# An attention and expert kernel on one core: scores and values in offset groups, and a new order at both ends

## What is computed

```python
scores = einsum('bhpqd,bhpkd->bhpqk', qb[:, :, rows], kb[:, :, cols]) * HEAD_DIM ** -0.5
ob = einsum('bhpqk,bhpkd->bhpqd', softmax(scores), vb[:, :, cols])
acc = segment_sum(ob, rows)
x = x + acc @ Wo.T
```

```python
masked = xf[None] * one_hot(argmax(softmax(xf @ gate_w.T))).T[:, :, None]
h = relu(einsum('end,edh->enh', masked, w1) + b1)
routing_output = (einsum('enh,ehd->end', h, w2) + b2).sum(0)
shared = relu(xf @ sw1 + sb1) @ sw2 + sb2
```

## Time and profile before

| | us |
|---|---|
| median of three runs | 916.06 |
| lowest, highest | 911.68, 916.23 |
| the profiled execution | 914.49 |
| its span, first to last instruction | 912.7 |
| TensorE busy in the span | 798.9 (88%) |
| VectorE busy | 593.8 (65%) |
| ScalarE busy | 497.3 (54%) |
| POOL busy | 429.5 (47%) |

### The profile page before, as it was taken

How to read it: one execution, slowest core, us unless ns; L and a number is a source line. 1 busy time by engine, 2 the same in 40 slices (tenths; PEclk the granted TensorE clock), 3 DMA queues, 4 the chain that set the end, 5 groups by cost and what they waited for, 6 DMA issues and landing times.

```text
span 912.7 us, 24404 instructions
## 1 busy us (share of the span) xinstructions
PE 798.9 (88%) x8374; PEld 665.8 (73%) x8374; DVE 593.8 (65%) x1248; ACT 497.3 (54%) x1150; POOL 429.5 (47%) x780
## 2 busy tenths in 40 slices
PE   3465777788999999999999999999999999989894
PEld 3333756577886869697878788787879697868794
DVE  4457577576757777685858676767677686745331
ACT  2264453636565575746575656556574756465452
POOL 2667333342536364554536363637364554455311
PEclk8576998999999999999999999999999999999997
DMA  6669221263624544544535353444444444414730
GB/s 193 185 194 304 69 86 35 81 206 96 199 79 123 161 138 144 159 141 140 170 115 196 114 166 125 145 140 136 161 128 151 149 144 136 148 49 140 239 109 23
DMA packets 97387, 128.19 MB, mean 140 GB/s; under 512 B 14655, under 2 KB 82623, under 8 KB 97088
## 3 DMA queue, kind: packets, MB, share of 16 engines
q1 hardware_dynamic: 89760, 107.89, 38.4%
q0 software_dynamic: 6624, 18.95, 6.2%
q10 hardware_dynamic: 960, 0.79, 0.4%
HBM read 90.80 MB, written 37.04 MB: 140 GB/s over the span
## 4 chain that ended last, share of the span: by engine, by line
PE 62%; DVE 14%; DMA 9%; issue 4%; ACT 4%; POOL 2%; SPq 2%; ACTq 1%; DVEq 0%; POOLq 0%
PE hid L533 16%; PE acc L724 14%; PE nd L638 11%; PE work L533 6%; PE work L622 5%; DVE nmax L1176 4%; PE work L666 3%; DVE PT L1219 2%; PE work L589 2%; DMA QP<-scratch_m 2%; DVE T L1192 2%; DVE check L1187 1%; DMA scratch_q<-T 1%; PE work L542 1%; DMA scratch_m<-mT 1%
## 5 line engine op out<-in xcount | busy, mean ns | idle before, releaser
L1442 POOL TENSOR_TENSOR hl<-h,hh 128x256 fp32r<-128x256 f32 x228 | 169.0, 744 | 326.1 <-ACT hh L982 325.9
L966 ACT ACTIVATE PT<-work 128x512 f32<-128x512 f32 x192 | 106.3, 605 | 55.6 <-PE work L622 55.5
L1195 DVE RECIPROCAL T<-nd 128x256 f32<-128x256 f32 x51 | 89.4, 1753 | 37.9 <-PE nd L638 32.8
L724 PE MATMUL acc<-w_hi,hh 128*128 128x256 f32 (+1 forms) x528 | 112.5, 295 | 0.0
L982 ACT ACTIVATE h<-hid,bias 128x256 f32<-128x256 f32 x144 | 69.1, 480 | 74.7 <-PE hid L533 74.7
L533 PE MATMUL hid<-Xs,W 128*128 128x256 f32 x816 | 109.6, 288 | 0.2
L533 PEld LDWEIGHTS hid<-Xs,W 128*128 128x128 f32 x816 | 102.9, 195 | 2.6 <-DVE Xs L1129 0.7
L724 PE MATMUL acc<-w_lo,hh 128*128 128x256 f32 (+1 forms) x528 | 104.7, 280 | 0.0
L533 PE MATMUL hid<-Xr,W 128*128 128x256 f32 x768 | 104.1, 285 | 0.0
L533 PEld LDWEIGHTS hid<-Xr,W 128*128 128x128 f32 x768 | 94.1, 188 | 5.1
L638 PE MATMUL nd<-PT,V 128*32 128x256 f32 x1024 | 84.0, 401 | 11.5 <-DVE T L1192 5.3
(11 more groups left out here) (191 smaller groups left out, 1651.5 us busy)
## 6 DMA issues: line engine op xcount, KB each, us to landing
W<-w1q SPq DMA_DIRECT2D x64, 512.0 KB, 5.8
KP<-scratch_k SPq DMA_DIRECT2D x192, 64.0 KB, 2.4
QP<-scratch_q SPq DMA_DIRECT2D x180, 64.0 KB, 2.3
scratch_k<-T SPq DMA_DIRECT2D x16, 512.0 KB, 3.5
scratch_q<-T SPq DMA_DIRECT2D x16, 512.0 KB, 3.2
yt<-yq SPq DMA_DIRECT2D x17, 260.0 KB, 2.8
xt<-xq SPq DMA_DIRECT2D x17, 256.0 KB, 3.8
xin<-x SPq DMA_DIRECT2D x16, 256.0 KB, 3.5
```

The source lines that it names most:

```text
L724: mm = nc.tensor.matmul(acc[:, t, :], R(h[:, u % 2, a, P * t:P * t + P]), R(row), start=first, stop=u == UNITS - 1 and h is hl and a == 1, ...
L966: nc.scalar.activation(PT[:, j % 4].rearrange("p t q -> p (t q)"), score_bank(j), ACT.Exp).then_inc(sem["exp_done"], 1)
L1195: nc.vector.reciprocal(T[:, p, :], nd[:, p % 2, 1, :]).then_inc(sem["inverted"], 1)
L1442: nc.gpsimd.tensor_tensor(R(hl[:, u % 2, a]), h32[:, u % 2, a], hh[:, u % 2, a], ALU.subtract).then_inc(sem["hl_done"], 1)
```

## The change

In iterations with a tile, scores and values come in groups: the scores of pairs 2g+1 and 2g+2, then a half of an expert, then the values of pairs 2g and 2g+1. The head sum is done in two halves, the first before the down half that it followed, the second between the two score visits of the next iteration. `ranks` goes behind `shared_down(n, 1)`.

In iterations 0 to 2: the context split of sequence 1 goes ahead of the weight splits; `SPLITS_AT` has another place, in iteration 1, with the last four pieces, which use slots 2, 3, 4, 3; pieces 5, 7 and 9 have their low half made by VectorE; TensorE waits for pieces 6 and 7 in place of all 24 ahead of iteration 1, and for the last one ahead of the first `table`; `make_constants` goes behind quotient 3, and TensorE waits for the load of the constants; `shared_up(n, 3)` goes ahead of the query projection, with its relu; `table` goes behind `front_v`; SP's residual load goes behind the spreads.

At the tail: the load of the tile's tokens goes behind the second of four weight loads (it was last), and `finish_shared` ahead of one `last_low`.

```diff
-SPLITS_AT = (4, 0, 0, 0, 0, 2, 2, 1, 1, 1, 1, 1, 1, 1, 1, 3, 5)
-SLOTS = [n % STAGES for n in range(W1_PIECES + W2_PIECES)]
+SPLITS_AT = (4, 0, 0, 0, 0, 4, 2, 1, 1, 1, 1, 1, 1, 1, 1, 2, 0, 4)
+ON_VECTOR = (5, 7, 9)
+SLOTS = [n % STAGES for n in range(W1_PIECES + W2_PIECES - 4)] + [2, 3, 4, 3]
...
         def low_done(n):
-            return sem["stage_lo"], n + 1
+            return (sem["stage_lo_dve" if n in ON_VECTOR else "stage_lo_pool"],
+                    sum((m in ON_VECTOR) == (n in ON_VECTOR) for m in range(n + 1)))
...
                     load_w1(W1[:, 1], expert, u)
-                    if u == 0 and not at:
+                    if u == (1 if at else 0):
                         sp.wait_ge(sem["x_queued"], 32 * (m + 1))
                         load_tile_x(m, row)
...
-                if at:
-                    sp.wait_ge(sem["x_queued"], 32 * (m + 1))
-                    load_tile_x(m, row)
...
-                if type(i) is int and i == 0:
-                    sp.wait_ge(sem["consts_read"], 1)
-                    load_residual(0, first=True)
-                else:
+                if tile:
                     load_residual(i)
...
                         spread(half)
+                if type(i) is int and i == 0:
+                    sp.wait_ge(sem["consts_read"], 1)
+                if not tile:
+                    load_residual(i, first=type(i) is int and i == 0)
...
                     if type(i) is int and i == 0:
-                        pe.wait_ge(sem["consts_read"], 1)
+                        pe.wait_ge(sem["consts_loaded"], 16 * 9)
...
+            def attention_out(i, more, c):
+                bank = claim(i, ("at", 0), more) if c == 0 else work[:, BANK["at", 0], :]
...
                 pe.wait_ge(sem["y_done"], e + 1)
+                if e == 0:
+                    pe.wait_ge(*low_done(len(pieces) - 1))
...
                 if shared:
+                    shared_down(n, 1)
                     ranks(n, claim(i, ("rk", 0), tile=tile))
-                    shared_down(n, 1)
...
                     expert = None
+                    if shared:
+                        shared_up(n, 3)
                 if more:
                     front_project(i + 1, "q", 0, a_hi, a_lo, "xT_lo", tile=tile)
...
-                elif shared:
-                    shared_up(n, 3)
                 scores_t(i, 0, more)
-                for p in range(PAIRS):
-                    if not tile and p % 2:
+                for p in range(0 if tile else PAIRS):
+                    if p % 2:
                         fill(n, m, tile, (p + 1) // 2, expert)
                     if p + 1 < PAIRS:
                         scores_t(i, p + 1, more)
-                    if tile and p % 2 == 0 and (more or p > 2):
-                        fill(n, m, tile, p // 2, expert)
                     values(i, p)
+                for group in range(GROUPS if tile else 0):
+                    for p in (2 * group + 1, 2 * group + 2):
+                        if p < PAIRS:
+                            scores_t(i, p, more)
+                    if more or group > 1:
+                        fill(n, m, tile, group, expert)
+                    values(i, 2 * group)
+                    values(i, 2 * group + 1)
+                attention_out(i, more, 0)
                 if tile:
                     tile_down(m, 1, expert)
-                elif shared:
-                    table(i - 1)
-                attention_out(i, more)
-                if more:
+                    if more:
+                        scores(i + 1, 0)
+                attention_out(i, more, 1)
+                if more and tile:
+                    scores(i + 1, 1)
+                elif more:
                     visit(i + 1, 0)
...
                     front_v(i + 1)
+                if shared and not tile:
+                    table(i - 1)
...
             iteration(0, False, False, True)
-            pe.wait_ge(*low_done(len(pieces) - 1))
+            pe.wait_ge(*low_done(6))
+            pe.wait_ge(*low_done(7))
...
             def splits(i, k):
-                if type(i) is int and i == 0:
+                if type(i) is int and i == (k == 17):
                     for n in slot_pieces(k):
                         split_high(n)
...
-                if more and not shared:
-                    context_high(i + 1)
+                    if u == 1:
+                        splits(i, 17)
...
+                elif shared:
+                    shared_relu(n, UNITS - 1)
                 splits(i, 6)
...
             front_v(0, acc[:, :, :])
+            context_high(1)
             for n in slot_pieces(0):
                 split_high(n)
...
+            def split_low(n):
+                dve.wait_ge(sem["stage_hi"], n + 1)
+                _, hi, lo = pieces[n]
+                nc.vector.tensor_tensor(R(lo), stage(n, lo), hi, ALU.subtract).then_inc(sem["stage_lo_dve"], 1)
...
+                if type(i) is int and i == 0:
+                    split_low(ON_VECTOR[0])
+                    split_low(ON_VECTOR[1])
                 if more:
                     front_q(i + 1)
                 if type(i) is int and i == 0:
-                    make_constants()
+                    split_low(ON_VECTOR[2])
...
                     divide(i, p)
...
+                    if type(i) is int and i == 0 and p == 3:
+                        make_constants()
...
+            finish_shared(last)
             last_low(tile_unit(last, 0), 0)
-            finish_shared(last)
...
             def split_and_load(n):
-                split_low(n)
+                if n not in ON_VECTOR:
+                    split_low(n)
...
-                if more:
+                splits(i, 17)
+                if more and shared:
                     context_low(i + 1)
...
                 load(n)
+            context_low(1)
             for n in slot_pieces(0):
                 split_and_load(n)
```

More of the change, by code:

```diff
@@ L114 @@
     "table_hi level_hi "
-    "bias_summed consts_made consts_read proj_lo ln1_step ln1_done ln2_step ln2_done xT_lo q_lo k_lo "
+    "bias_summed consts_made consts_read proj_lo stage_lo_dve ln1_step ln1_done ln2_step ln2_done xT_lo q_lo k_lo "
     "max_done m_lo inverted checked t_done at_lo x1_done gate_step masked ranked x2_lo xr_lo y_done r_done "
     "level_sum level_made ids_moved last_low "
-    "zeroed stage_lo veps1_done veps2_done rstd1_done rstd2_done c_lo hl_done table_lo "
+    "zeroed stage_lo_pool veps1_done veps2_done rstd1_done rstd2_done c_lo hl_done table_lo "
     "place_step placed left_made pad_made"
@@ L641, in values @@
                 mm.then_inc(sem["pv_done"], 1)
[L643 to L654, removed]
+            def attention_out(i, more, c):
+                bank = claim(i, ("at", 0), more) if c == 0 else work[:, BANK["at", 0], :]
+                bank = bank.rearrange("p (c t) -> p c t", c=DC)
+                pe.wait_ge(sem["t_done"], PAIRS * i + 4 * c + 4)
+                for r in range(NBLK):
+                    queries = slice(BLOCK * r, BLOCK * r + BLOCK)
+                    for q in range(4):
+                        mm = nc.tensor.matmul(bank[32 * q:32 * q + 32, c, queries], hsum[:, r, :],
+                                              T[:, 4 * c + q, queries], start=True, stop=True)
+                if c == DC - 1:
+                    mm.then_inc(sem["at_full"], 1)
             def project_out(i, more):
@@ L1045, in iteration @@
                     tile_relu(m, 1)
-                elif shared and not tile:
-                    shared_relu(n, UNITS - 1)
                 exps(i, 0)
@@ L1536, in split_low @@
                 _, hi, lo = pieces[n]
-                nc.gpsimd.tensor_tensor(R(lo), stage(n, lo), hi, ALU.subtract).then_inc(sem["stage_lo"], 1)
+                nc.gpsimd.tensor_tensor(R(lo), stage(n, lo), hi, ALU.subtract).then_inc(sem["stage_lo_pool"], 1)
             def split_and_load(n):
-                split_low(n)
+                if n not in ON_VECTOR:
+                    split_low(n)
                 if SLOTS[n] in SLOTS[n + 1:]:
```

## The result

The changed kernel takes 920.22 us (median of 20 runs, 914.47 to 925.62) and the kernel before 915.78 (20 runs, 911.12 to 918.73): ratio 1.0056, 95% interval 1.0035 to 1.0077, about 5 us slower. The forecast was 914.0, no change that counts.

A forecast was written before the change was run, and what follows sets the result against it. TensorE was taken as the bound, busy 563.6 of 585 us at full clock in the tile iterations. Terms +7.8 - 0.5 - 2.3 - 3.0 - 4.0 = -2.0 gave 914.0 us against the 916.06 median; range 903 to 924.

The forecast's parts named there:

- the tail: After the tile iterations: earlier token load saves 2.6 us, earlier finish_shared 1.4; together -4.0, ends -1 and -4.4.
- Tile iterations: Twelve iterations with a tile of routed tokens: +0.65 us each from grouping, head sum and ranks, together +7.8.
- Groups +1.4: Joined scores and values in each tile iteration: new waits outweigh savings, +1.4 us, ends -1.05 and +2.0.
- pair 2's 1.3: First group of a tile iteration: pair 2's scores wait 1.3 us for exponentials of pair 0, whose banks they take.
- pair 4's 0.15: Second group: other TensorE work covers all but 0.15 us of pair 4's wait for pair 2's exponentials.
- pair 6's 0.7: Third group: pair 6's scores wait 0.7 us because F1's relu precedes pair 4's exponentials on ScalarE.
- The joins: Tile iterations: joining saves 0.21 us per pair of scores and 0.14 per pair of values, at most 1.05 per iteration.
- Ranks -0.5: Tile iterations: shared_down(1) covers the 0.77 us mask wait, late maxima then limit it; -0.5, ends 0 and -0.77.
- Head sum -0.25: Tile iterations: splitting it covers 0.34 us more of the last-quotient wait, less 0.1; -0.25, ends 0 and -0.7.
- Rival B: Faster: only pair 2 waits, groups cost +0.7, full mask gain; total -9.8, 906 us, chance 0.35.
- Rival C: Slower: the new 1.3 us wait drops the clock, costing 1.5 us per affected iteration; 926 at eight, chance 0.22.
- Front: Iterations 0 to 2: -2.3 us up to iteration 1's key projection, -3.0 in the rest of iterations 1 and 2.

The follow-up runs named there:

- the second execution: Both kernels run once more, unchanged, one profiled execution each: the kernel before 913.17 us, the changed kernel 927.12 us.
- the tail alone: The kernel before with only the tail's two moves (token load ahead of two weight loads and the bias, finish_shared one unit earlier): ratio 1.0031.

## Why the prediction was wrong

**The step that failed is the tail**: "The two weight loads behind it come some 6 us later, needed later still. -2.6. finish_shared one unit earlier: the 1.5 for yp, -1.4. Together **-4.0**". Alone it measured +2.8, outside its ends of -1 and -4.4, a miss of 6.8 us. Put 2.8 in its place and the sum of the prediction is +4.8 instead of -2.0; measured were 5.1 by the ratio.

The wait for yp is gone, as forecast. The wait for the tokens shrank from 2.88 to 1.90 only, 1.0 for a forecast of 2.6, and "under 1" was missed. The scatter ahead of the load was to land sooner under half the weights; it took 6.48 instead of 6.95, and the load itself 2.87 instead of 3.35. From the chain that ended last, changed kernel:

```profile
854.23 6.48 DMA xq<-xhat,pos
...
860.86 2.87 DMA xt<-xq
```

That alone would have left a gain of about 2.5. What turned it into a loss, and what I did not count, is what stands next on the sync queue. SyncE's queue in the kernel before:

```profile
855.82 0.38 SPq L370 DMA_DIRECT2D xt<-xq  x1
857.03 0.42 SPq L486 DMA_DIRECT2D xq<-T  x1
...
862.09 1.79 SPq L366 DMA_DIRECT2D W<-w1q  x4
864.14 0.39 SPq L370 DMA_DIRECT2D xt<-xq  x1
```

and in the changed kernel:

```profile
860.86 0.38 SPq L372 DMA_DIRECT2D xt<-xq  x1
861.43 0.85 SPq L368 DMA_DIRECT2D W<-w1q  x2
862.47 0.33 SPq L399 DMA_DIRECT2D bsel<-b  x1
863.63 0.42 SPq L486 DMA_DIRECT2D xq<-T  x1
...
869.33 2.14 SPq L368 DMA_DIRECT2D W<-w1q  x4
871.73 0.44 SPq L372 DMA_DIRECT2D xt<-xq  x1
```

The second token load goes out 8.32 us after the first before and 10.87 after: two weight loads and the bias now stand between them, ahead of the padding writes and the four weight loads that stood there already. In the changed kernel it goes out about 0.2 after the last padding write has landed, which took 4.3 instead of 2.7; before, that write had landed over 1 us earlier. Its landing, from the transfers by issue (KB each, us to landing), in the kernel before:

```profile
xt<-xq SPq DMA_DIRECT2D x1, 256.0 KB, 6.7
```

and in the changed kernel:

```profile
xt<-xq SPq DMA_DIRECT2D x1, 256.0 KB, 8.3
```

Before, the tokens landed at 870.81 and were used at 871.60: 0.8 to spare (0.7 in the second execution). That was in the trace before the change, and it means that of any gain ahead of that point only 0.8 could be kept unless the tokens landed earlier too. Counted from the first transposes they now land 4.7 us later (16.29 instead of 11.59), while TensorE arrives 1.5 us earlier (10.87 instead of 12.38). It waits 5.46 and then runs at the lower clock: from the second transposes to the third 14.47 us instead of 12.07, 2.4 more. With the tokens ahead of the weights, in the tail alone, the wait is gone. The transfer there:

```profile
xt<-xq SPq DMA_DIRECT2D x1, 256.0 KB, 2.8
```

Its issue comes only 0.8 us sooner than in the tail alone without that edit (67.82 for 68.59 after the maxima of iteration 15); the landing, 2.8 instead of 7.7 after it, is what the place in the queue is worth. Whether that comes from the order in the queue or from the 2 MB of weights in flight at the same time, no run tells apart.

**Tile iterations: right in sum, with luck.** +0.65 was forecast, +0.56 measured.
- Groups +1.4: measured 1.24 in the iteration shown, 1.27 by the periods (49.33 against 48.06), 14.8 us by the runs. The waits have the causes named, but are smaller: pair 2's 1.3 was 1.01, pair 4's 0.15 nothing, pair 6's 0.7 was 0.56, 1.57 for 2.15. The joins save less too, some 0.3 for 1.05: two pairs of values do take 1.86, but two pairs of scores in a row, pairs 3 and 4, take 0.94 (520.69 to 521.63), where two single ones took 0.44 and 0.43. So joining scores saved nothing. And the forecast's three net terms, redone from its own waits and savings, are 1.05, -0.20 and +0.35: 1.20, not 1.4. These errors cancel; that the sum is near is luck.
- Ranks -0.5: 0.54. Head sum -0.25: 0.24. Both by one profile each; the runs don't confirm them.
- Rival B (only pair 2 waits) falls: the relu of F1 does hold pair 6.

**Rival C happened in one iteration of twelve, in the second execution in two.** Iteration 3 takes 2.9 us longer, 1.6 more than the groups account for. TensorE in time, changed kernel, iteration 3:

```profile
216.89 0.59 PE L622 MATMUL work<-QP,KP 56*128 56x256 f32 x5 [0.82 <-DMA QP<-scratch_m]
...
218.63 0.50 PE L622 MATMUL work<-QP,KP 56*128 56x256 f32 x4 [1.00 <-ACT PT L981]
```

Here the scores have also waited 0.82 for the rows of the maxima, 1.7 us before the wait of 1.00, and the clock is 0.50 from 221 to 223. The four other profiles with this grouping (three with another front or tail, and the second execution) show the same in iteration 3: waits of 0.54 to 1.19 ahead, then 1.00, and 0.50 to 0.52 in a stretch of 2 us. In the eleven iterations of these five profiles the wait of 1.01 or 1.02 stands alone 50 times, and the clock stays at 1.00; five times one of 0.15 to 0.24 stands ahead of it, and once of these the clock falls. The price forecast for it, 1.5, was right (1.6 in iteration 3, 1.7 in the second execution's other one).

**Front: right in sum.** -5.3 was forecast, -6.0 measured by the runs; the two profiles show 4.4 (2.4 at the maxima of iteration 3, and the 2.06 of the first transfers). Where it lies: from the first maxima to the first score visit of iteration 1 it takes 48.58 us (37.31 to 85.89) instead of 54.78 (35.25 to 90.03), 6.2 less for a forecast of 7.5. (The forecast's own terms, 8.9 removed and 2 and 2 given back, are 4.9; the rest of the 7.5 had only VectorE's norm named for it.) The wait for c_lo of 6.07 is gone there, but TensorE now waits 4.57 instead of 1.50 for VectorE's a_lo. VectorE's three ops on the constants take 2.17 (64.81 to 66.98) for a forecast of 2.0. Then iteration 1 gives 4 back for a forecast of 5.2 (20.07 to 24.09 us from that visit to its first transposed scores), by the cause named. POOL in time, changed kernel:

```profile
96.62 0.59 POOL L1558 DMA_DIRECT2D yt<-w  x1 [0.30 <-POOL w_lo L1563]
97.24 1.27 POOL L1563 TENSOR_TENSOR w_lo<-xt,w_hi 128x512 fp32r<-128x512 f32 x1
100.24 1.26 POOL L1563 TENSOR_TENSOR w_lo<-yt,w_hi 128x512 fp32r<-128x512 f32 x1 [1.73 <-ACT w_hi L975]
101.46 1.26 POOL L1453 TENSOR_TENSOR c_lo_t<-ctx_in,c_hi_t 128x512 fp32r<-128x512 f32 x1
```

The last piece holds POOL until 101.46, c_lo follows, and the key projection starts at 102.87 after 3.03 of wait, not after over 5: the transposed maxima ahead of it waited 2.35 themselves. From the key projection to the maxima of iteration 3 it takes 106.13 instead of 108.34, 2.2 less for a forecast of 3.0: the waits for scratch_q and those of 2.40 ahead of the token transposes are gone, and the last quotient, which the table no longer covers, is waited for 2.73 and 2.72.

Of VectorE's three weight splits two, with no split of POOL running, took 0.68 and 0.69; one, begun at 49.94 under a POOL split of 49.77 to 51.06, took 1.67. The trace agrees here with the Trainium skill's rule ("SBUF — State Buffer", "Who interferes with whom"). Of the loss of up to 4 us this shows 1.0 on VectorE.

## To carry to other kernels

Before a wait is priced as a gain, ask of the next transfer on the same queue when it lands and how much it has to spare; its issue and landing are in the trace, and a gain ahead of it is capped by that slack. Joining work of one kind (here the values, 0.14 a join) pays only while something else covers the buffer that comes back: keep a long piece of other work between the first and the second use of a bank. A part that costs may hide one that pays: undone singly, this change held 10 us of gain under 15 of loss, and the half between the scores with the next tokens first runs at 0.9757 of the kernel before (892.78 us).

## What was not expected

Two short waits close together lowered the clock where one of about the same length had not: 0.82 and 1.00 us, ending 1.7 us apart, against 1.01 or 1.02 alone, 50 times at clock 1.00 in the five profiles with this grouping. Where the border lies is not shown: 0.21 and 1.02 lowered it once, 0.24 and 1.01 did not. And the 256 KB of the next tile's tokens took 6.6 to 8.3 us to land behind four weight loads of 512 KB, in all nine profiles with that order, and 2.6 to 4.2 in the nine with the tokens ahead of them.
